# Attention and FFN block on one Trainium2 core: splits and products in another order, and the low weight halves of the output projection made by an accumulating DMA

## The reference

```python
x = x + attention(layernorm(x), ctx, ctx, mask, Wq, Wk, Wv, Wo)
x = x + ffn(layernorm(x))

# attention: 32 query heads, 8 key/value heads (4 query heads share one), head size 128, 16 blocks of 128 tokens
q, k, v = x @ Wq, ctx @ Wk, ctx @ Wv          # Wq 1024x4096, Wk and Wv 1024x1024
q, k = rope(q), rope(k)
logits = 30 * tanh(q @ k.T * 0.0884 / 30)
weights = softmax(where(mask, logits, -1e30))
out = (weights @ v) @ Wo                      # Wo 4096x1024

# ffn: base product with bias, and rank 16 adapters of the two best of 8 experts
base = x @ W_base.T + b_base
out = base + lora(x, top2(x @ W_router.T), A, B) * 2
```

## Time and profile before

| what | value |
|---|---|
| runs (3) | median 2184.87 us, 2184.8 to 2186.41 |
| the profiled execution | 2188.56 us, its span 2186.8 us |
| TensorE busy | 2139.8 us, 98% |
| VectorE busy | 1625.3 us, 74% |
| ScalarE busy | 870.0 us, 40% |
| GpSimd busy | 782.0 us, 36% |
| DMA | 508.52 MB, 233 GB/s in the mean |

### The profile page before, as it was taken

How to read it: one execution, slowest core, us unless ns; L and a number is a source line. 1 busy time by engine, 2 the same in 40 slices (tenths; PEclk the granted TensorE clock), 3 DMA queues, 4 the chain that set the end, 5 groups by cost and what they waited for, 6 DMA issues and landing times.

```text
span 2186.8 us, 26557 instructions
## 1 busy us (share of the span) xinstructions
PE 2139.8 (98%) x9429; PEld 1729.0 (79%) x9429; DVE 1625.3 (74%) x2059; ACT 870.0 (40%) x1351; POOL 782.0 (36%) x764
## 2 busy tenths in 40 slices
PE   9989999999999999998999999999999999999999
PEld 7778887878787888886777777877777777888887
DVE  4767667889877666675687789898989888855533
ACT  3223333222232111126555556665665566423211
POOL 0281015556623000003442256445645554624300
PEclk9999999999999999999999999999999999999999
DMA  8679666776667555658755585568556864586851
GB/s 292 215 223 312 212 215 231 271 269 257 249 252 288 200 205 201 237 199 287 244 192 188 193 299 172 187 244 310 184 193 232 289 226 164 183 331 244 316 227 67
DMA packets 198532, 508.52 MB, mean 233 GB/s; under 512 B 20864, under 2 KB 46080, under 8 KB 196352
## 3 DMA queue, kind: packets, MB, share of 16 engines
q1 hardware_dynamic: 172160, 424.43, 54.8%
q0 software_dynamic: 26240, 82.38, 11.2%
HBM read 357.26 MB, written 149.16 MB: 232 GB/s over the span
## 4 chain that ended last, share of the span: by engine, by line
PE 82%; DVE 8%; issue 4%; DMA 4%; ACT 1%; POOL 1%; SPq 0%; DVEq 0%; ACTq 0%; POOLq 0%
PE pq L235 27%; PE pq L237 26%; PE pq L236 26%; PE pq L1283 1%; DMA kD<-kst 1%; DVE kRl L520 1%; DVE qW L880 1%; DVE Rl L1213 1%; DVE ql L1365 1%; DMA kraw<-ctxT 1%; DVE Y L1471 1%; DMA QSD<-qW 0%; DVE Al L1458 0%; POOL Pl L1520 0%; DMA RB<-rD 0%
## 5 line engine op out<-in xcount | busy, mean ns | idle before, releaser
L235 PE MATMUL pq<-Ah,Rh 128*128 128x512 f32 x1024 | 399.8, 390 | 3.5 <-DVE Y L1471 1.8
L236 PE MATMUL pq<-Al,Rh 128*128 128x512 f32 x1024 | 398.6, 389 | 0.0
L237 PE MATMUL pq<-Ah,Rl 128*128 128x512 f32 x1024 | 398.6, 389 | 0.0
L1213 DVE TENSOR_TENSOR Rl<-raw,Rh 128x1024 fp32r<-128x1024 f32 x176 | 279.2, 1587 | 120.7 <-ACT Rh L1208 120.3
L235 PE MATMUL pq<-Xq,qW 128*128 128x512 f32 x896 | 351.7, 392 | 16.1 <-issue 4.7
L237 PE MATMUL pq<-Xq,qW 128*128 128x512 f32 x896 | 350.6, 391 | 0.0
L236 PE MATMUL pq<-Xq,qW 128*128 128x512 f32 x896 | 350.3, 391 | 0.0
L1208 ACT ACTIVATE Rh<-raw 128x1024 fp32r<-128x1024 f32 x176 | 184.8, 1051 | 154.2 <-PE pq L237 114.5
L1526 POOL DMA_DIRECT2D r<-rT x32 | 22.9, 717 | 589.7 <-ACT rT L1394 589.7
L235 PEld LDWEIGHTS pq<-Ah,Rh 128*128 128x128 f32 x1024 | 192.2, 188 | 48.0 <-DVE Y L1471 2.8
L237 PEld LDWEIGHTS pq<-Ah,Rl 128*128 128x128 f32 x1024 | 192.2, 188 | 40.6
(11 more groups left out here) (244 smaller groups left out, 4204.2 us busy)
## 6 DMA issues: line engine op xcount, KB each, us to landing
raw<-gran SPq DMA_DIRECT2D x177, 512.0 KB, 4.5
QSD<-qW SPq DMA_DIRECT2D x64, 512.0 KB, 3.3
qD<-qt SPq DMA_DIRECT2D x128, 256.0 KB, 4.4
qW<-QSD SPq DMA_DIRECT2D x64, 512.0 KB, 3.4
qf<-qD SPq DMA_DIRECT2D x64, 512.0 KB, 6.4
RB<-rD POOLq DMA_DIRECT2D x128, 256.0 KB, 4.7
qraw<-gran SPq DMA_DIRECT2D x48, 512.0 KB, 5.0
kD<-kst SPq DMA_DIRECT2D x32, 512.0 KB, 5.4
```

Source lines behind the costliest of these rows:

```text
L235: e.matmul(dst, lh, rh, start=first, stop=False, skip_group_check=more)
L236: e.matmul(dst, lh, rl, start=False, stop=False, skip_group_check=more)
L237: return e.matmul(dst, ll, rh, start=False, stop=last, skip_group_check=more)
L1213: t.e.tensor_tensor(l, raw[raw_of(x)][:, :], f(h), ALU.subtract).then_inc(*t.tick("w_lo", x))
```

## The change

Nine edits, in the order of the stages.

1. KV: `act_kv` makes the high halves of pieces before the kst copies, the square roots and the diagonals. `DIAG`, `SPREAD` and `SUMS` of the later chunks come some jobs later. `pool_kv` waits for the low half of V piece 15 before its step (2, 0).
2. KV to Q: SP loads Xq4 before Xq3, and Xq3 is split at step NK - 2. The first fresh products of a bank wait for the V job that used it, not for the last one.
3. Q: the products of a round come in the order 0, 1, 4, 3, 2, 5, 6, rounds 14 and 15 with it. Post-addition 4 is made when both 3 and 4 are through.
4. Q: `X_POOL` gives GpSimd 18 instead of 21 low halves of Xq; VectorE makes those of Xq6 one product later.
5. Q: the rotation of round 31 comes in two parts (it was one).
6. Q to attention: the first loads of q, k and v wait for product (31, 2), not (31, 3), and `load_qk(0)` is issued at NU - 3, as the last products now stand.
7. O: for pieces 12 to 139 ScalarE writes the negated high half into the low slot (`w_neg`), and GpSimd issues a DMA that adds the raw weights from DRAM to it (`w_add`); VectorE's difference is gone.
8. O: TensorE waits for that DMA (`w_done`), and a raw buffer is free when the high half is made.
9. In each step GpSimd issues its `w_add` first.

```diff
-        DIAG = {15: 0, 16: 1, 34: 2, 35: 3}
-        SPREAD = {..., 37: (2, 0), 38: (2, 1), 39: (3, 0), 40: (3, 1)}
+        DIAG = {15: 0, 16: 1, 38: 2, 39: 3}
+        SPREAD = {..., 41: (2, 0), 42: (2, 1), 43: (3, 0), 44: (3, 1)}
-        SUMS = {25: (0, 0), 26: (0, 1), 28: (0, 2), 30: (0, 3)}
+        SUMS = {25: (0, 0), 26: (0, 1), 33: (0, 2), 35: (0, 3)}
-        QP = [(n, i) for n in range(14) for i in range(7)]
-        QP += [(14, 0), (14, 1), (14, 2), (15, 0), (14, 3), (15, 1), (14, 4), (15, 2), (14, 5), (15, 3), (14, 6), (15, 4), (15, 5), (15, 6)]
-        QP += [(n, i) for n in range(16, 32) for i in range(7)]
+        QP = [(n, i) for n in range(14) for i in (0, 1, 4, 3, 2, 5, 6)]
+        QP += [(14, 0), (14, 1), (14, 4), (14, 3), (15, 0), (14, 2), (15, 1), (14, 5), (15, 4), (14, 6), (15, 3), (15, 2), (15, 5), (15, 6)]
+        QP += [(n, i) for n in range(16, 32) for i in (0, 1, 4, 3, 2, 5, 6)]
@@ act_kv: the loop over p moves from behind DIAG to ahead of the kst copies
+                for p in range(NPC):
+                    if pc_at[p] == n:
...
+                        e.activation(h, place, ACT.Copy).then_inc(*t.tick("kv_hi", p))
@@ pool_kv
+                    if (k, i) == (2, 0):
+                        t.wait_ge("kv_lo", piece_of["W", 15])
@@ sp_q_early, X_SPLIT
-                x_load(t, 0, n - NK + 10)
+                x_load(t, 0, 4 if n == NK - 7 else 3)
-        X_SPLIT = {42: 0, 44: 1, 48: 2, NK - 5: 3, NK - 3: 4}
+        X_SPLIT = {42: 0, 44: 1, 48: 2, NK - 3: 4, NK - 2: 3}
@@ pe_q
-                    t.wait_ge("kv_vl", len(v_jobs) - 1)
+                    job = {(0, 0): 49, (0, 1): 51, (0, 4): 50, (1, 0): 53, (1, 1): 55, (1, 4): 54}[n, i]
+                    t.wait_ge("kv_vl", v_of[KJ[job][1:]])
-        X_POOL = [(0, 1, 2, 3)] * 4 + [(0, 1, 2), (0, 1), ()]
+        X_POOL = {0: (0, 1, 2, 3), 1: (0, 1, 2), 4: (0, 1, 2), 3: (0, 1, 2), 2: (0, 1, 2), 5: (0, 1), 6: ()}
@@ TURN
-            d = 6 if n == 31 else 2 if n in (13, 14) else 1
+            d = 3 if n == 31 else 2 if n in (13, 14) else 1
@@ dve_q
-                if 0 < u <= NU and QP[u - 1][1] in (1, 3, 4, 5, 6):
-                    q_post(t, *QP[u - 1])
+                if 0 < u <= NU:
+                    n, i = QP[u - 1]
+                    if i in (1, 3, 5, 6):
+                        q_post(t, n, i)
+                    if i in (3, 4) and max(q_number[n, 3], q_number[n, 4]) == u - 1:
+                        q_post(t, n, 4)
-                if 0 <= u - 4 < NU and QP[u - 4][0] == 15:
-                    x_low(t, 1, QP[u - 4][1], [k for k in range(4) if k not in X_POOL[QP[u - 4][1]]])
+                for i, lag in ((0, 4), (1, 4), (4, 4), (3, 4), (2, 4), (5, 4), (6, 5)):
+                    if u == q_number[15, i] + lag:
+                        x_low(t, 1, i, [k for k in range(4) if k not in X_POOL[i]])
@@ w_load
-                t.wait_ge("w_lo", FILL[i - RAW])
+                if FILL[i - RAW] == "bt" or not by_dma(FILL[i - RAW]):
+                    t.wait_ge("w_lo", FILL[i - RAW])
@@ w_high and new functions
-            t.e.activation(piece(x)[1], raw[raw_of(x)][:, :], ACT.Copy).then_inc(*t.tick("w_hi", x))
+            src, h, l = piece(x)
+            t.e.activation(h, raw[raw_of(x)][:, :], ACT.Copy).then_inc(*t.tick("w_hi", x))
+            if by_dma(x):
+                t.wait_ge("w_hi", x)
+                t.e.activation(l, f(h), ACT.Copy, scale=-1.0).then_inc(*t.tick("w_neg", x))
+        def by_dma(x):
+            return 12 <= x < 12 + 128
+        def w_done(t, x):
+            if x != "bt" and by_dma(x):
+                t.wait_ge(f"d_wl{(x - 4) % RING}", x)
+            else:
+                t.wait_ge("w_lo", x)
+        def w_add(t, x):
+            src, h, l = piece(x)
+            t.wait_ge("w_neg", x)
+            t.e.dma_start(l, src, accum_op=ALU.add).then_inc(*t.tick(f"d_wl{(x - 4) % RING}", x, 16))
@@ pe_att
-                    t.wait_ge("w_lo", x)
+                    w_done(t, x)
@@ dve_step (both places)
-            for x in [y for y in SPLIT.get(at, []) if at >= 0]:
+            for x in [y for y in SPLIT.get(at, []) if at >= 0 and not by_dma(y)]:
@@ pool_step, first of all
+            for x in SPLIT.get(at, []):
+                if by_dma(x):
+                    w_add(t, x)
@@ load_qk and load_v
-                t.wait_ge("q_pe", (31, 3))
+                t.wait_ge("q_pe", (31, 2))
@@ sp_att_early
-            if u == q_number[31, 4]:
+            if u == NU - 3:
                 load_qk(t, 0)
```

More of the change, by code:

```diff
@@ L41 @@
     "prep": ("kv_dg", "kv_dgl", "kv_bn", "kv_rs", "kv_mask", "kv_xb", "set", "q_xl0", "q_xl2"), "kv_low": ("kv_kl", "kv_vl", "v_vl"),
-    "kv_high": ("kv_kh", "kv_vh", "v_vh"), "prep_act": ("kv_sq", "kv_dgh", "kv_x"), "p": ("a_exp", "a_ph"),
+    "kv_high": ("kv_kh", "kv_vh", "v_vh"), "prep_act": ("kv_sq", "kv_dgh", "kv_x", "w_neg"), "p": ("a_exp", "a_ph"),
     "top": ("f_lg", "f_m8", "f_ix", "f_pr", "f_ixf", "f_oh", "f_w", "f_wx", "f_r2"), "f_act": ("f_e", "f_h", "f_hwh"),
@@ L465, in act_kv @@
                                  scale=1.0 if i else -1.0).then_inc(*t.tick("kv_x", (c, i)))
+                for p in range(NPC):
+                    if pc_at[p] == n:
+                        src, place, h, l, s, after, first = PC[p]
+                        if after:
+                            t.wait_ge(*after[0:2])
+                        t.wait_ge(s, p)
+                        e.activation(h, place, ACT.Copy).then_inc(*t.tick("kv_hi", p))
                 if 0 <= n - 2 < NK and KJ[n - 2][0] == "K" and KJ[n - 2][3]:
@@ L482, in act_kv @@
                         e.activation(high[:, :], whole[:, :], ACT.Copy).then_inc(*t.tick("kv_dgh", (c, i)))
[L483 to L489, removed]
                 if 0 <= n - 1 < NK and KJ[n - 1][0] == "V":
@@ L1035, in program @@
         for n in range(32):
-            d = 6 if n == 31 else 2 if n in (13, 14) else 1
+            d = 3 if n == 31 else 2 if n in (13, 14) else 1
             for x in range(0, 6, d):
-                TURN.setdefault(q_number[n, 6] + 1 + x // d, []).append((n, tuple(range(x, x + d))))
+                TURN.setdefault(q_number[n, 6] + (1 if n == 15 else 1) + x // d, []).append((n, tuple(range(x, x + d))))
         TURNED = {}
         for n in range(32):
-            TURNED.setdefault(q_number[n, 6] + (4 if n in (13, 14, 31) else 7), []).append(n)
+            TURNED.setdefault(q_number[n, 6] + (4 if n in (13, 14, 31) else 7 if n == 15 else 7), []).append(n)
         def dve_q(t):
             for u in range(NU + 7):
-                if 0 < u <= NU and QP[u - 1][1] in (1, 3, 4, 5, 6):
-                    q_post(t, *QP[u - 1])
+                if 0 < u <= NU:
[4 more added lines that the diff above has]
+                        q_post(t, n, 4)
                 for x, ahead, i in ((0, 7, 1), (1, 6, 1), (2, 6, 3), (3, 7, 6)):
@@ L1471, in dve_step @@
                 e.tensor_tensor(Y[:, m, :], ps[ring_bank(n)][:, :], Y[:, m, :], ALU.add).then_inc(*t.tick("y_add", n))
-            for x in [y for y in SPLIT.get(at, []) if at < 0]:
+            for x in [y for y in SPLIT.get(at, []) if at < 0 and not by_dma(y)]:
                 w_low(t, x)
@@ L1667, in pool_att_early @@
             return
-        EARLY_X = {q_number[31, 2] + x: x for x in range(4)}
+        EARLY_X = {NU - 5 + x: x for x in range(4)}
         LN_LOAD, LN_MEAN, LN_SQUARE, LN_SPLIT, LN_RSTD, LN_MORE, LN_OUT = 4, 8, 15, 25, 30, 36, 38
```

2 lines of the change are left out of this document (1 added, 1 removed).

## The result

The changed kernel takes 2276.43 us (median; 2273.45 to 2280.8), the kernel before beside it 2184.84 us (2183.97 to 2186.41): a ratio of 1.042, 95% interval 1.0402 to 1.0438. The change costs 91.6 us. 2170 was forecast, with a range of 2152 to 2194.

What follows compares the result with a forecast made beforehand. TensorE, busy for 98%, was taken as the bound, losing time to waits and clock dips. KV -14.4, Q -5.3, O's start +5 and steady O 0 made -14.7 us; with the run median 3.7 lower: 2170, range 2152 to 2194.

Steps and rivals of the forecast that it cites:

- Net 0: O's steady part: 2 us lost in layer norm stretches against 2 us of waits for Y won.
- 1.8 + q: O's steady part: RB's lateness, 1.8 us plus q behind the accumulate in the queue; q taken as 2.
- 4.9 us: O's steady part: how late RB may be before TensorE's sums wait for the exp, allowing q up to 3.1.
- O's start: First O pieces: TensorE stands 6.1 us, clock dip 1.6 more, loss 7.7 (bounds 4 and 11); net 5 us slower.
- B: Rival, O: RB late in every group through GpSimd's queue, 58 us, 2228, chance 0.11; mild form 2185, chance 0.10.
- C: Rival, O: DMA engines saturate, from 1.7 plain loads per accumulate on; the 800 us become 840, 2210; chance 0.05.
- softmax and RB catch up: O's start: while TensorE stands, the 1.7 us at 1051 and about 1 beside go.
- I cost this at nothing: KV: GpSimd's wait delays normalisation, sums and Xq loads; no cost, or a K piece late by 1 to 3 us.
- D: Rival, KV gives half: fourth V piece waits for kst's store or a K piece is late; 2177 to 2182, chance 0.14.
- 627 and 674: Q stalls: product (15,0) comes later, 1.3 us won; post 3 stands ahead of Xq6's lows, 2.0 of 3.8 won.
- what is won at the front is lost there: net 0: Q's start: first product starts sooner, sixth waits behind Xq6's loads; net 0 (bounds -1.7 and +1.5).
- the scattered stalls of rounds 2 to 13 stay: Q: distances 1 to 3 and 3 to 5 and VectorE's work per round stay; bounds 3 us either way.

Runs made afterwards that it cites:

- kvq_only: The changed kernel with its K, V and Q edits only, O's low halves left to VectorE as before: 2165.81 us, ratio 0.9912.
- add_eighth: The changed kernel with each accumulate cut to the first 128 of 1024 columns, leaving out the rest of the subtraction: 2179.68 us, ratio 0.9981.
- half_odd: The changed kernel with only odd pieces, from piece 17 on, by accumulate, the others by VectorE: 2207.73 us, ratio 1.0109.
- add_last: The changed kernel with the accumulate's issue moved from the front of GpSimd's step to behind broadcast, Pl and gather: 2213.78 us, ratio 1.0132.
- rec_late: The changed kernel with VectorE's reciprocal one step later, behind that step's sum into Y: 2237.41 us, ratio 1.0244.
- small_sp: The changed kernel with the gather, rD and RB issued from SyncE at its step's end instead of from GpSimd: 2232.05 us, ratio 1.0207.
- sp_rec_late: The changed kernel with `small_sp`'s SyncE issues and `rec_late`'s later reciprocal together: 2217.39 us, ratio 1.0156.
- half_even: The changed kernel with only even pieces, from piece 16 on, by accumulate, the others by VectorE: 2254.59 us, ratio 1.031.
- from16: The changed kernel with pieces 12 to 15 of O left to VectorE and accumulates from piece 16 on: 2258.14 us, ratio 1.0342.
- plain_load: The changed kernel with each of the 128 accumulates replaced by a plain GpSimd load, the subtraction left out: 2216.8 us, ratio 1.0126.

## Why the prediction was wrong

**What failed is the steady part of O**, forecast as "Net 0": it cost 89 us. Two figures in it were off, and one wait was missing. The table gives medians over groups of the time from the start of the copy of the sums (rT) to the start of the first product with RB, and the mean distance of two groups, worked out from the starts in each trace. Groups 2 to 9 lie ahead of the first layer norm, 10 to 30 mostly beside one.

```
              groups 2-9            groups 10-30
              rT to RB  distance    rT to RB  distance
before          16.0     27.87        19.05    28.62
kvq_only        16.1     27.88        18.8     28.62
add_eighth      18.1     28.00        20.0     29.16
half_odd        18.1     28.63        20.3     29.84
add_last        18.0     28.31        19.6     30.05
rec_late        20.0     29.10        21.9     30.56
small_sp        16.0     29.02        19.3     30.72
sp_rec_late     16.0     28.36        17.9     30.25
half_even       22.3     30.51        22.7     32.00
changed         21.7     29.15        23.3     32.38
```

- The lateness. Only RB was made late in my sum, by 1.8 + q = 3.8 us. q = 2 was right: from issue to product 5.4 us became 7.2. But three transfers stand in the chain. The gather got late too (4.3 became 5.8 us from its issue to the reciprocal), and so did rD and the broadcast's issue. In all 5.6 us in groups 2 to 9.
- The slack. 4.9 us was read in one group, around 1208 us, ahead of the first layer norm. In the kernel before, the groups beside layer norm already take 3.0 us more (19.05 against 16.0), so that by my estimate some 2 us (4.9 less 3.0) were left of it where most groups lie; 4.5 came (23.3 against 18.8). I took the DMA share of such a stretch for its tightness; it wasn't what was tight.
- The wait that I didn't list. I asked what is queued behind the accumulate for RB and not for the gather: VectorE's reciprocal waits for it in order, ahead of Y. Moving it is worth 39 us (`rec_late`), the layer norm operation that the wait pushed beside GpSimd's work with it. `small_sp` and `sp_rec_late` show that RB's lateness is not all: RB is at most 0.5 us late there, and the groups beside layer norm are still 2.1 and 1.6 us longer than in `kvq_only`, with waits for the gather of up to 14.2 and 9.7 us.

The price: 21 groups by 3.76 us and 8 by 1.27 us are 89 us; with O's start at 18 this is 107 of the 110.6 us between the changed kernel and `kvq_only`, and the 4.8 us that lie before matmul 4000 are about the rest.

**The rivals.** B, on the slower side, was the mechanism: GpSimd's queue at the broadcast's step, 2 us in each of 29 groups, 2228. It came with 3.1 us per group, since the gather came on top, and with a dearer start of O. Its sign, TensorE waiting for Pf at its sums, is there 16 times in 32 groups (20.1 us in all), and the waits for Y behind it on VectorE, which B didn't name, are 31.9 us. C, full DMA engines, is half right. An accumulate passes C's threshold of 1.7 loads: queue q0's 26.5% of 2275.1 us less 11.2% of 2186.8 us, by 16 engines, are 5727 engine-us, 44.7 for each of 128; the same bytes on q1 took 23.6 (45 per MB, 0.524 MB), so 1.9 loads; against a plain load out of GpSimd's own queue (26.5, below) it is 1.7. The share in 1100 to 1900 us rose to 0.93. But a full share alone cost nothing (`add_last`, 453 matmuls at 1.01); Rl landed in 8.0 us, not in over 15. The extra time acts through whoever is queued behind: with plain loads, of 26.5 engine-us by the same working (q0 20.6% of 2216.4 us), 60 us of the loss went, and with another order, 63.

The two source reads of the Trainium skill, *Collectives: The Full Stack*, section "The bandwidth ceiling: the fold count and why AG ≠ RS ≠ AR", told there of a collective's add, agree with the 1.7 to 1.9 loads; its conclusion that the doubled traffic is the bottleneck does not carry over to this kernel, by the 453 matmuls at a share of 1.01.

**O's start.** I had a wait of 6.1 us, 1.6 for the clock and 2.7 regained. ScalarE's copies and the issue came as costed (negative ready at 1014.4, issued at 1014.73), but the first accumulate landed 8.6 us after its issue, where I had 6, and TensorE stood 8.4 us instead of 6.1. The granted clock was at the 1.2 GHz level for 10.2 us after 1017.8 (0.60 over 1020 to 1030). TensorE stood for the first 5.5 of them; the 11 matmuls in the other 4.7 cost 2.4 us, where I had taken 1.6. And "softmax and RB catch up" was wrong: the store of the reciprocals (rD), issued 0.6 us behind the fourth accumulate, landed after 11.1 us (3.7 in the kernel before), so RB was issued at 1035.75 only and TensorE stood 4.3 us more for the exponentials. Nothing was regained. The start is worth 18 us by the medians of `from16`; its trace has 3.1 of the difference already before matmul 4000. GpSimd's issues, then TensorE's stretch and its second wait:

```profile
1014.73 0.92 POOL L1237 DMA_DIRECT2D Rl<-gran  x1
...
1035.75 2.15 POOL L1543 DMA_DIRECT2D RB<-rD  x4 [10.50 <-DMA rD<-r]
```

```profile
1020.00:1030.00 10.00, 6.60 (x19) 0.60 1.05 274
```

```profile
1044.80 1.60 PE L1312 MATMUL pq<-Pf,ones 128*32 128x512 f32 x2 [4.33 <-ACT Pf L1429]
```

**KV.** Right at the places costed. From the table by matmuls: by matmul 500 the lead is 9.1 us, 6.3 of it at the stall of 101 to 108 (5.2 forecast; 2.8 were there by matmul 300, from smaller waits). At 150 to 158 another 8.2 came (7.9), and 1.4 at 317 (1.3). Wrong was "I cost this at nothing" for GpSimd's later Yx work: by matmul 700 7.9 us were gone again, and the lead at the end of KV was 9.1 us instead of 14.4. The earlier trace rows had shown both halves of it, a VectorE difference stretched to over 4 us beside GpSimd, and I asked only about this difference. D's loss came, but by another way: its sign, waits for kRl, stayed away (four differences from 138.9 on, 1.23 us at most), and the loss stood at the mask.

**Q.** 3.3 us were forecast up to matmul 4000 (627 and 674) and 2.0 behind it. `kvq_only` gains 15.3 from matmul 1345 to 4000 (23.3 less 8.0), the changed kernel 9.4. In `kvq_only` the start won 2.6 ("what is won at the front is lost there: net 0"), 627 won 1.4 (1.3), and 674 and what follows won 4.2 (2.0). The largest part was in the rounds between, which I had left as they were ("the scattered stalls of rounds 2 to 13 stay", 3 us either way): 7.1 from matmul 1500 to 2500, half of it at one stall at 584 us; the changed kernel had a wait of 4.5 us there again and kept 2.4. Behind matmul 4000 `kvq_only` won 2.1 more by matmul 4400 (2.0 for 987). At matmul 4000 the changed kernel's 18.5 us stand against 17.7 forecast for KV and Q up to there: right by two errors that cancel, 5 us too much in KV and 6 too little in Q.

## What to carry to other kernels

A change that moves work to a DMA is priced not by its bytes alone but by what is queued behind it: list every small transfer of the same issuer that a loop waits for, with its slack, and read this slack in the tightest stretch, not in a convenient group. In an engine's order, a wait costs what stands behind it; putting the wait for a late transfer one step later, or the large transfer behind the small ones, was worth 39 and 63 us here with the same work. And where GpSimd's or VectorE's SBUF work moves in time, by an edit or by a late transfer, look at what the other does in the new place.

## What the runs showed of the hardware

- An accumulating DMA of 0.52 MB took 44.7 engine-us, a plain GpSimd load of it (`plain_load`) 26.5, and a SyncE load 23.6, each by its queue's share.
- A broadcast issued from SyncE landed in 4.7 us while accumulates ran in the software queue; in the same queue with them, 7.8 in the median.
- GpSimd's issue of an accumulate took 0.89 us in the median (0.85 to 1.16), RB's four 2.50 us at 1464.22 (2.14 before).
- A DMA share of 1.01 went with TensorE at full pace, 453 matmuls in 100 us (`add_last`).
- A VectorE operation with two SBUF inputs took 5.4 to 6.9 us beside GpSimd's work, five times, where it took 0.6 in `kvq_only`.
